# A two-layer image block on one Trainium2 core: the order of work inside a scan chunk is drawn anew

## The reference, cut to what matters

```python
dts = jnp.einsum('bkrl,kdr->bkdl', dts, dt_w)
delta = jax.nn.softplus(dts + dt_b[None, :, :, None])
def step(h, xs_t):
    d_t, u_t, B_t, C_t = xs_t
    dA = jnp.exp(d_t[..., None] * A)
    h = h * dA + (d_t * u_t)[..., None] * B_t[:, :, None, :]
    y = jnp.einsum('bkdn,bkn->bkd', h, C_t)
    return (h, y)
```

## Time and profile before

| what | value |
|---|---|
| median of 3 runs | 14318.21 us (14317.18 to 14324.84) |
| the profiled execution | 14321.17 us, span 14319.4 us |
| busy over the span | PE 85%, DVE 85%, ACT 85%, POOL 69% |
| mean granted TensorE clock | 0.974 |
| DMA | mean 103 GB/s |

### The profile page before, as it was taken

The page is one execution under the profiler, slowest core; times in us unless marked ns, Lnnn a source line. Parts: engine busy times, 40 slices in busy tenths (PEclk is TensorE's granted clock), DMA queues, the critical chain, the costliest instruction groups (busy, mean ns, idle before and its releaser), DMA issues.

```text
span 14319.4 us, 281562 instructions
## 1 busy us (share of the span) xinstructions
PE 12173.0 (85%) x71128; PEld 7344.9 (51%) x71128; DVE 12205.0 (85%) x13653; ACT 12188.8 (85%) x28586; POOL 9892.3 (69%) x4006
## 2 busy tenths in 40 slices
PE   6887988889888898888988889888898888988889
PEld 4554555545555455554555545555455554555545
DVE  8999779997799967999679986899858998599985
ACT  6998789987889878998889978899788997889978
POOL 5999069980699807998079970899708996099960
PEclk9999999999999999999999999999999999999999
DMA  3443024440344303443034430344303442044420
GB/s 117 134 134 125 28 95 132 134 127 22 101 132 133 121 22 106 133 142 105 22 115 132 143 98 22 120 133 143 91 22 128 132 142 85 22 134 132 142 79 27
DMA packets 908190, 1470.82 MB, mean 103 GB/s; under 512 B 38912, under 2 KB 891904, under 8 KB 893664
## 3 DMA queue, kind: packets, MB, share of 16 engines
q1 hardware_dynamic: 906560, 1452.37, 32.1%
HBM read 1350.07 MB, written 102.17 MB: 101 GB/s over the span
## 4 chain that ended last, share of the span: by engine, by line
PE 31%; issue 29%; ACT 15%; POOL 14%; DVE 9%; ACTq 1%; DVEq 0%; DMA 0%; POOLq 0%; SPq 0%
POOL area L1652 11%; PE ps L710 9%; DVE area L1110 6%; ACT ps L1430 5%; PE ps L946 4%; PE ps L927 4%; ACT area L1385 4%; PE ps L688 4%; PE ps L697 2%; POOL area L1662 2%; POOL area L1641 1%; PE ps L792 1%; DVE area L360 1%; ACT hst L1353 1%; PE ps L736 1%
## 5 line engine op out<-in xcount | busy, mean ns | idle before, releaser
L1110 DVE TENSOR_TENSOR_SCAN area<-ps,area 128x385 f32<-128x385 f32 x9216 | 8102.7, 940 | 312.1 <-ACT ps L1430 266.5
L1652 POOL TENSOR_TENSOR area<-area 128x1152 f32<-128x1152 f32 x3072 | 7995.3, 2638 | 45.7 <-POOL area L1641 45.7
L1430 ACT ACTIVATE ps<-area,a_neg 128x384 f32<-128x384 f32 x9216 | 5110.6, 579 | 334.9 <-DVE area L1110 311.8
L710 PE MATMUL ps<-area,ident 128*128 128x384 f32 x10368 | 3905.7, 509 | 332.1 <-POOL area L1662 207.6
L688 PE MATMUL ps<-ident,area 128*128 128x128 f32 x12096 | 2114.9, 284 | 1352.7 <-ACT area L1385 1348.5
L710 PEld LDWEIGHTS ps<-area,ident 128*128 128x128 f32 x10368 | 1909.7, 197 | 1814.1 <-ACT area L1409 401.7
L1385 ACT ACTIVATE area<-ps,area 128x384 f32<-128x384 f32 x4032 | 2310.2, 573 | 536.5 <-PE ps L688 536.1
L688 PEld LDWEIGHTS ps<-ident,area 128*128 128x128 f32 x12096 | 1388.8, 141 | 2614.3 <-ACT area L1385 2048.3
L1595 ACT ACTIVATE area<-ps,t_neg,area 128x384 f32<-128x384 f32 x3456 | 2127.7, 668 | 111.2 <-PE ps L927 23.6
L1636 POOL TENSOR_TENSOR area<-area,ones 128x2304 f32<-128x2304 f32 x8 | 43.6, 5446 | 3067.6 <-ACT area L1333 2947.9
L697 PE MATMUL ps<-ident,area 128*128 128x128 f32 x12096 | 2027.4, 277 | 131.0 <-ACT area L1385 129.9
(11 more groups left out here) (142 smaller groups left out, 10552.7 us busy)
## 6 DMA issues: line engine op xcount, KB each, us to landing
area<-bc_rows SPq DMA_DIRECT2D x1536, 768.0 KB, 6.7
xz<-x_normed SPq DMA_DIRECT2D x144, 288.0 KB, 3.6
area<-in_x SPq DMA_DIRECT2D x18, 1728.0 KB, 10.1
area<-x_padded SPq DMA_DIRECT2D x24, 1250.0 KB, 5.8
z_raw<-z_st SPq DMA_DIRECT2D x144, 192.0 KB, 2.8
area<-z_raw SPq DMA_DIRECT2D x8, 3456.0 KB, 12.6
x_padded<-x_st SPq DMA_DIRECT2D x120, 200.0 KB, 7.3
x_normed<-area SPq DMA_DIRECT2D x9, 1728.0 KB, 7.9
```

The lines of the kernel that those rows point to most:

```text
L710: m = e.matmul(ps[:, 5 + j, 0:CH], ident[:], hb[i % NH][:, j], start=i == 0, stop=i == N - 1)
L1110: e.tensor_tensor_scan(track(HB, i, j, k), rev(ps[:, 2 + j, side(k):side(k) + WIDE], k), track(DBU, i, j, k), 0.0, ALU.mult, ALU.add).then ...
L1430: e.activation(ps[:, 2 + j, 1:1 + CH], dlt[:, par, j], ACT.Exp, scale=a_neg[:, j, k, i:i + 1]).then_inc(da, 1)
L1652: e.tensor_tensor(dbu[i % NH], du[:, par], row_b[:, q % 2, i % ROWS:i % ROWS + 1].broadcast_to([128, J, CH]), ALU.mult).then_inc(dbus, 1)
```

## The change

The states are dealt out anew: GpSimd multiplies states 0 and 9 by C, VectorE 2, 5, 8, 11, 13 and 15, and eight states are turned (1, 3, 4, 6, 7, 10, 12, 14), with a new table of slots. Delta's bias becomes one more row of TensorE's weights `w_dt`, against a row of ones that `dt_rows` makes by adding 1 to that partition; the copy with the bias goes, abs reads PSUM, ln writes SBUF, and the steps of the softplus move to earlier states. `head` does two states at once. On ScalarE the second turned product of a slot moves behind the three exponentials, the first behind the second exponential, and `c_copy` of state i moves from the end of step i+1 to behind the first exponential of step i+2. On TensorE, `delta_tile` and `unit` move from ahead of a slot to behind its first turn and the turned sum after it.

```diff
-POOL_N = (0, 4, 9)
-TURN_N = (1, 3, 6, 7, 10, 12, 13)
-TURN_AT = {2: (0,), 3: (1, 2), 4: (3, 4), 5: (5,), 7: (6, 7), 8: (8, 9), 9: (10, 11), 11: (12, 13), 12: (14,),
-           13: (15, 16), 14: (17, 18), 15: (19, 20)}
+POOL_N = (0, 9)
+TURN_N = (1, 3, 4, 6, 7, 10, 12, 14)
+TURN_AT = {2: (0,), 3: (1, 2), 4: (3,), 5: (4, 5), 6: (6, 7), 7: (8, 9), 8: (10, 11), 9: (12, 13), 10: (14,),
+           11: (15, 16), 12: (17,), 13: (18, 19), 14: (20,), 15: (21, 22), 16: (23,)}
-SUM_AT = {0: 3, 2: 4, 4: 6, 5: 7, 8: 10, 9: 12, 11: 13, 14: 16, 15: 17}
+SUM_AT = {0: 3, 2: 4, 5: 7, 8: 10, 9: 12, 11: 13, 13: 15, 15: 17}
-SOFT = ((3, "abs", 0), (4, "exp", 0), (5, "ln", 0), (6, "abs", 1), (7, "exp", 1), (8, "ln", 1),
-        (9, "abs", 2), (10, "exp", 2), (11, "ln", 2))
+SOFT = ((2, "abs", 0), (2, "exp", 0), (3, "ln", 0), (5, "abs", 1), (5, "exp", 1), (6, "ln", 1),
+        (8, "abs", 2), (8, "exp", 2), (9, "ln", 2))
+STEP_AT = {2: 0, 5: 1, 8: 2}
-UNIT_AT = (10, 14)
+UNIT_AT = (10, 13)
...
                     if before:
                         turned_sum(g, before[-1])
+                    if between:
+                        between()
                     for i in SUM_ORDER:
                         if SUM_AT[i] == m and i in DVE_N:
                             state_sum(g, i)
...
+                        def between():
+                            j = DELTA_AT.get(m) if nxt else None
+                            if j is not None:
+                                e.wait_ge(hcs, gd + (1, 2, 3)[j])
+                                delta_tile(*nxt, j, 1)
+                            if k < UK and m in UNIT_AT:
+                                unit(k, h, gd, UNIT_AT.index(m))
...
-                    e.wait_ge(carry, g * 16 + (i + 1))
+                    e.wait_ge(carry, g * 16 + (i + 2))
-                    e.activation(slot[:, :, 0 if k < 2 else CH], hst[:, i], ACT.Copy).then_inc(heads, 1)
+                    e.activation(pair[:, :, :, 0 if k < 2 else CH], hst[:, i:i + 2], ACT.Copy).then_inc(heads, 1)
...
-                    if len(now) == 1 and j == 1:
+                    if now and j == 1:
                         turned_product(g, k, c, now[0])
-                    if len(now) == 2 and j != 1:
-                        turned_product(g, k, c, now[j // 2])
+                    if len(now) == 2 and j == J:
+                        turned_product(g, k, c, now[1])
...
+                            if j == 0 and i > 1:
+                                c_copy(g, i - 2, nxt, h)
...
-                        if i >= 1:
-                            c_copy(g, i - 1, nxt, h)
...
+            e.wait_ge(consts, 16 * len(loads))
+            for k in range(K):
+                e.dma_start(w_dt[DT0[k] + R:DT0[k] + R + 1, k].rearrange("o (j p) -> o j p", j=J),
+                            t["b_dt"][:, :, k:k + 1].rearrange("p j o -> o j p"),
+                            allow_slow_non_contiguous=True).then_inc(bias_row, 16)
```

More of the change, by code:

```diff
@@ L711, in state_sum, with slot @@
                     m.then_inc(ysum, 1)
-                def slot(g, m):
+                def slot(g, m, between=None):
                     for i in SUM_ORDER:
@@ L743, in body @@
                     for m in range(N):
-                        j = DELTA_AT.get(m) if nxt else None
-                        if j is not None:
-                            e.wait_ge(hcs, gd + (1, 2, 3)[j])
-                            delta_tile(*nxt, j, 1)
-                        if k < UK and m in UNIT_AT:
-                            unit(k, h, gd, UNIT_AT.index(m))
-                        if m < 2 and last:
-                            slot(g - 1, N + m)
+                        def between():
[5 more added lines that the diff above has]
+                                unit(k, h, gd, UNIT_AT.index(m))
                         if m == 3 and not last:
@@ L754, in body @@
                             e.wait_ge(ct_cp, b * GM + GM)
-                        slot(g, m)
+                        if m < 2 and last:
+                            slot(g - 1, N + m, between)
+                            slot(g, m)
+                        else:
+                            slot(g, m, between)
                         if m in ADD_AT:
@@ L1056, in delta @@
                 e.wait_ge(dp_a, g * 9 + SOFT_N["ln", j])
-                e.scalar_tensor_tensor(out=dlt[:, par, j], in0=dlt[:, par, j], scalar=0.0, in1=ps[:, bank, 0:CH],
+                e.scalar_tensor_tensor(out=dlt[:, par, j], in0=ps[:, bank, 0:CH], scalar=0.0, in1=du[:, par, j],
                                        op0=ALU.max, op1=ALU.add).then_inc(dp_v, 1)
@@ L1120, in body @@
                             times_c(g, i - 1)
-                        if nxt and i in LN_AT:
-                            delta(g + 1, 1 - par, LN_AT[i])
+                        if nxt and i in STEP_AT:
+                            delta(g + 1, 1 - par, STEP_AT[i])
                 def times_c(g, i):
@@ L1299, in _, with softplus @@
             group_std(1, 0)
-            def softplus(g, par, k, op, j, bank=1, h=None):
-                x, y = dlt[:, par, j], du[:, par, j]
-                if op == "x":
+            def softplus(g, par, op, j, bank=1):
+                y = du[:, par, j]
+                if op == "abs":
                     e.wait_ge(dp_mm, g * 3 + (j + 1))
-                    e.activation(x, ps[:, bank, 0:CH], ACT.Identity, bias=b_dt[:, j, k:k + 1]).then_inc(dp_rd, 1)
-                elif op == "abs":
-                    e.wait_ge(dp_rd, g * 3 + (j + 1))
-                    e.activation(y, x, ACT.Abs).then_inc(dp_a, 1)
+                    e.activation(y, ps[:, bank, 0:CH], ACT.Abs).then_inc(dp_a, 1)
                 elif op == "exp":
@@ L1314, in softplus @@
                     e.wait_ge(dp_a, g * 9 + SOFT_N["exp", j])
-                    if bank == 1 and j < 2:
-                        e.wait_ge(dp_rd, g * 3 + (j + 2))
-                    if bank == 1 and j == 2:
-                        e.wait_ge(hcs, g * ND + (1 + DVE_N.index(8) + 1 - ND))
-                    if h is not None:
-                        e.wait_ge(unit_ev, h * 2 + 1)
-                    e.activation(ps[:, bank, 0:CH], y, ACT.Ln, bias=1.0).then_inc(dp_a, 1)
+                    e.activation(y, y, ACT.Ln, bias=1.0).then_inc(dp_a, 1)
             def dt_rows(b, o, c):
@@ L1325, in dt_rows @@
                 e.activation(dts[64 - 64 * o:128 - 64 * o, c * CH:(c + 1) * CH], ps[64:128, xp_bank(o, c), 0:CH],
-                             ACT.Copy).then_inc(xp_ev, 1)
+                             ACT.Identity, bias=dt_one[64:128]).then_inc(xp_ev, 1)
             def front(b):
@@ L1339, in front @@
                 dt_rows(b, 0, 1)
-                for j in range(J):
-                    softplus(g0, 0, 0, "x", j, 5 + j)
                 for n, (_, op, j) in enumerate(SOFT):
@@ L1425, in body @@
                     for i in range(N):
-                        if nxt and i == 3:
+                        if nxt and i == 2:
                             e.wait_ge(dbus, g16 + 8)
@@ L1454, in body @@
                             unit_out(h, UNIT_AT.index(i - 1))
-                        if nxt and i in LN_AT:
-                            softplus(g + 1, 1 - par, nxt[0], "ln", LN_AT[i], h=h if i == 11 else None)
-                        if i >= 1:
-                            c_copy(g, i - 1, nxt, h)
+                        if i < 2 and last:
+                            turned_products(g - 1, *last, N - 1 + i, J)
+                        turned_products(g, k, c, i - 1, J)
                         if i == 2 and last:
@@ L1463, in body @@
                             store_y(g - 1, *last, 0)
+                        if i == 3 and last:
+                            store_y(g - 1, *last, 2)
                         if nxt:
-                            for at, op, j in SOFT:
-                                if at == i and op != "ln":
-                                    softplus(g + 1, 1 - par, nxt[0], op, j)
+                            for at, op, d in SOFT:
+                                if i == 2 and d == 0 and not last or at == i and op == "exp" and (last or d):
+                                    softplus(g + 1, 1 - par, op, d)
                 walk(e, body)
@@ L1473, in scan_phase @@
                 c_copy(g, N - 1, None)
-                for at in turns(N - 1):
+                for at in turns(N - 1) + turns(N):
                     turned_product(g, K - 1, NC - 1, at)
```

66 lines of the change are left out of this document (35 added, 31 removed).

## The result

The changed kernel takes 15,180.08 us (median of 4 runs, 15,170.99 to 15,202.35), the kernel before on the same chips 14,317.69 (14,315.97 to 14,324.84): a ratio of 1.0604, 95% interval 1.0585 to 1.0622. It is 862 us slower, where the forecast was 582 and the range ended at +782. The direction was right, the size was not.

What follows compares the result with a forecast made beforehand. No engine bounds the whole; VectorE (50.4 us work) and GpSimd (51.4) nearly fill a 51.9 us chunk. Stalls lose 3.1 a chunk: 192 x 3.1 - 10 = +585, giving 14,900 us median, range 14,530 to 15,100.

Steps and rivals of the forecast that it cites:

- The mechanism: Scan stage: VectorE waits for C's row copies, ln and a state sum; ScalarE for delta's tile and turns; GpSimd under 90%.
- The walk: One direction 2 chunk traced through the changed instruction orders: 50.4 us of VectorE work plus 4.9 of stalls, 55.3.
- The step that failed: From one traced chunk to the mean: larger stalls may swallow irregular waits; loss 2.7 to 3.4 us a chunk, taken as 3.1.
- Three orders decide: Scan chunk: late C-row copy, delta's tile behind a turn, and crowded slots 12 to 15 cause 4.9 us of stalls.
- The copy with the bias is not on the path to the scans now: ScalarE's softplus in the scan chunk: removing three bias copies saves 1.4 us of its work, with scans not depending on them.
- delta's tile behind a turn: Slots 4 and 7: ScalarE stands 0.9 us in steps 5 and 8; VectorE stalls 0.7 and 1.4 at delta's steps.
- ScalarE gains three turned products (+1.4), loses three copies (-1.4): ScalarE's work in a scan chunk: three turned products and three bias copies at 0.46 us each cancel.
- GpSimd as the pace: Scan stage: GpSimd sets the pace; 2.3 us less work brings the chunk to about 51.1, 14,030 us; chance 0.12.
- VectorE quicker with GpSimd idle: Scans up to a tenth quicker with no GpSimd beside them, -0.2 us a chunk, 14,280 us; chance 0.01.
- Waits that only change places: Scan chunk: GpSimd's relief pays for the new waits; chunk stays 52.6, 14,318 us; chance 0.04.
- Only the third order bites: Only slots 12 to 15 stall (0.5 + 1.7 replacing 1.25): +1.0 to +1.8 a chunk, 14,510 to 14,660 us; chance 0.18.

Runs made afterwards that it cites:

- the short product: Kernel before with GpSimd's product of state 4 by C made over only the first 8 positions of each tile (y wrong): 14,315.08 us, ratio 0.9994.

## Why the prediction missed the size

**The mechanism, right.** Engines wait for each other's latencies and no engine's work sets the end. VectorE waits for the copy of C's row at states 4 and 15, for ln at two of delta's steps, ScalarE waits for delta's tile (385 us in 368 waits, some 1 us each) and for turns (857 against 536 us), GpSimd falls under 90%. All were forecast. GpSimd's products delta*u were to stand 55 to 56 us apart; they do where no low clock falls, and in the mean they stand 57.1 apart.

**The walk, nearly right in its sum.** It gave 55.3 for a chunk of direction 2, against 55.7 in those chunks that the clock leaves alone. Stall by stall, forecast and measured: 0.3 and 0.27 at state 4; 0.7 and 0.59 at the second step of delta; 1.4 and 1.27 at the third; 0.5 and 0.74 in front of state 13, though it waits for the copy of row 11 and not, as forecast, for the slot behind state 9's sum; 1.7 and 1.52 at state 15.

**The step that failed** is the one from the walked chunk to the mean: "Today's mean chunk is 52.6, 0.7 longer than the one I walked, partly by irregular waits that larger stalls may swallow, so the loss against today lies between 2.7 and 3.4; I take 3.1". I took 0.4 for what a mean chunk has beyond the walked one (52.6 + 3.1 - 55.3). Measured, the mean chunk is 57.1 by the 22 chunks from 3971.64 to 5228.19, so it has 1.4 beyond the undisturbed 55.7. The difference of 1.0 is 192 us; the walk's own 0.4 is 77 more; together 269 of the 280 us that were missing. Nothing was swallowed. Two things stand in its place. One is shown: TensorE's clock falls to 1.2 GHz behind its waits for the stores of y, and where every other chunk of direction 2 pays 1.2 us for it, matmuls with zero weights take that away and 91 us with it. Direction 3 shows it more strongly: the chunk without a low stretch takes 54.8 us, those with two or three 57.0 to 57.8, and with the extra matmuls all take 55.4 to 56.1. And the "irregular waits" of before come with the low clock too. In the chunk behind the walked one it fell behind waits for ScalarE:

```profile
4449.40:4451.40 2.00, 1.39 (x10) 0.93 (x9) 2.00 (x4) 2.00 (x7) 2.00 (x1) 0.94 0.69 180
4451.40:4453.40 2.00, 2.00 (x5) 1.03 (x4) 2.00 (x3) 1.54 (x5) 2.00 (x2) 0.50 0.00 0
4453.40:4455.40 2.00, 2.00 (x6) 1.17 (x5) 2.00 (x3) 0.58 (x1) 2.00 (x2) 0.71 0.00 0
```

TensorE, ScalarE and VectorE behind it:

```profile
4450.98 3.79 PE L710 MATMUL ps<-area,ident 128*128 128x384 f32 x6
...
4455.46 0.58 ACT L1306 ACTIVATE area<-ps,b_dt 128x384 f32<-128x384 f32 x1 [0.61 <-PE ps L676]
...
4460.64 0.96 DVE L1110 TENSOR_TENSOR_SCAN area<-ps,area 128x385 f32<-128x385 f32 x1 [0.40 <-ACT ps L1430]
...
4466.65 1.81 DVE L1110 TENSOR_TENSOR_SCAN area<-ps,area 128x385 f32<-128x385 f32 x2 [0.39 <-ACT ps L1430]
```

The state sum took 3.79 us, in the walked chunk 2.10; ScalarE waited for delta's tile, and VectorE twice for exponentials, where the walked chunk has one such wait, of 0.20. The chunk took 52.65 us (4449.46 to 4502.11), the walked one, in which the clock stayed at 1.00 throughout, 51.89. It is so in all chunks of this image in directions 0, 2 and 3, apart from the first of directions 0 and 2: eight without a low stretch take 51.5 to 51.9 us, seven with one 52.0 to 52.6. So the walk started from an undisturbed chunk, and what a low stretch adds had to be put on top of its sum, not taken off.

The Trainium skill ("TensorE: Matmul & The Clock Gate", Part 1) says that a clock gate lets all or half of the pulses through, by how busy the array has been. The windows here show the same two levels, 1.00 and 0.50. They do not show the rule at work: at 4680.80 and one chunk later TensorE's waits are the same, and only the first brings a fall.

The other is direction 1, whose chunks take 2.5 us more than those of direction 2 (1.2 before). With the extra matmuls they take 57.9, still about 2 more. Their windows show low stretches as well (the clock of the direction is 0.95, and with the extra matmuls each of its chunks still has one), but VectorE also waits there for state sums, in places where direction 2 has no such wait:

```profile
4364.25 2.66 DVE L1124 TENSOR_TENSOR_SCAN area<-ps,area 128x385 f32<-128x385 f32 x3 [0.80 <-PE ps L716]
...
4369.34 3.51 DVE L1124 TENSOR_TENSOR_SCAN area<-ps,area 128x385 f32<-128x385 f32 x4 [0.70 <-PE ps L716]
```

Part of it is not the clock: in the kernel with the paired heads alone the six chunks of direction 1 take 53.0 us each without any low stretch, 1.3 more than an undisturbed chunk of direction 2. How the rest divides in the changed kernel stays open, since no run separated the two.

**What was attributed wrongly.** "Three orders decide" was half true. They cost 436 us together; about 470 come from parts that I costed at nothing (197 and 270), less 45 from the heads. Two steps were wrong by themselves. "The copy with the bias is not on the path to the scans now" is correct and beside the point: the copy freed a PSUM bank. My walk had its effect in it, as the 1.4 at the third step of delta, and put it under "delta's tile behind a turn"; with the tile ahead of the slot, the wait for ln is still 349 us. And "ScalarE gains three turned products (+1.4), loses three copies (-1.4)" netted two edits of which neither is neutral: taking the copies away, with the softplus crowded, lost 270 us, and turning one state more lost 212. That the walk was right in sum all the same is because it walked the finished kernel. Two small things: GpSimd's work in the walked chunk adds up to 16 x 2.60 + 2.6 + 3 x 2.32 = 51.2 us, not 51.4, on which nothing hangs; and the 0.5 in front of state 13 came from another cause than forecast, so that its nearness to 0.74 is luck.

**The rivals.** GpSimd as the pace: refuted by the short product (0.9994), where nothing else changes; state 4 turned (+212) agrees. VectorE quicker with GpSimd idle: the scan takes 939 ns with GpSimd 62% busy and took 940 at 69%; the Trainium skill's rule of the shared port ("Perfetto Trace Analysis", Optimizing Scalar/DVE Operations) gives nothing to gain in this trace. Waits that only change places: no, they grew by 718 us. Only the third order bites: no, all three show in VectorE's waits, and the products' own part is 41 us of time, by a single run.

## What to carry to other kernels

Where four engines are each busy over 80% of a stage and hand work round in order, taking work off the busiest one can give nothing (here 2.1 us a chunk off GpSimd), and putting a little on the path that the others wait for can cost most of its time (here 212 us for 265 us of products); ask of each removed instruction what it also released (a bank, a slot), not only what it took. A walk through one period came within half a microsecond here, but it gives a sum, not a cause: single edits divide it, and what a mean period has beyond the walked one has to be looked at too, in a period that is longer. Time a change of many parts part by part; here one of the smallest was a gain of 45 us that the others hid.

## What the runs showed of the hardware

- A low stretch of TensorE's clock, even where VectorE waited for nothing while it lasted, cost the chunk time in both kernels: 0.8 us before (52.65 against 51.89), 1.2 after (56.86 against 55.66), by waits of VectorE up to 12 us behind it. Extra matmuls with zero weights, put into TensorE's own wait, cut such a wait from 1.15 to 0.21 us and made the kernel 91 us faster.
- A copy of six elements for each partition took the pitch of one of three, about 0.1 us (L1365 at 4683.92, the next instruction at 4684.02):

```profile
4683.82 0.20 ACT L1356 ACTIVATE hst<-area 128x3 f32<-128x3 f32 x1
4683.92 0.20 ACT L1365 ACTIVATE area<-hst 128x6 f32<-128x6 f32 x1
4684.02 0.48 ACT L1413 ACTIVATE area<-ps 128x384 f32<-128x384 f32 x1
```
